# Graph network kernel: fourteen instead of eight pairs of gathered rows before the attention message pass

## The reference, cut to what matters

```
h = x @ W.T                                    # 8 heads of 64
e = leaky_relu(e_src + e_dst) * (1 + et_emb[edge_type]) * edge_weight
e = exp(e - e_max[dst]);  alpha = e / (e_sum[dst] + 1e-10)
msg = h[src] * alpha[:, :, None]
out = zeros.at[dst].add(msg) + x               # then a layer norm
# third layer:
h_self  = x @ W_self.T
h_neigh = mean of x[src] by dst @ W_neigh.T
```

## Time and profile before

| | us |
|---|---|
| median of 3 runs | 1936.45 |
| lowest and highest run | 1935.54, 1938.03 |
| profiled execution, its span | 1934.6 |
| median above the profiled span | 1.85 |
| POOL busy in the whole span | 705.2 |
| POOL gathers for the pass (L693), 176 | 178.6 |
| stage of the attention weights, first POOL gather to last ScalarE copy | 1090.87 to 1134.45 |
| message pass, first ScalarE copy to last matmul | 1135.13 to about 1354.9 |

### The profile page before, as it was taken

The page is one execution under the profiler, slowest core; times in us unless marked ns, Lnnn a source line. Parts: engine busy times, 40 slices in busy tenths (PEclk is TensorE's granted clock), DMA queues, the critical chain, the costliest instruction groups (busy, mean ns, idle before and its releaser), DMA issues. The chain is left out here.

```text
span 1934.6 us, 27686 instructions
## 1 busy us (share of the span) xinstructions
PE 1608.4 (83%) x7565; PEld 981.3 (51%) x7566; DVE 1167.7 (60%) x2310; ACT 471.2 (24%) x884; POOL 705.2 (36%) x605
## 2 busy tenths in 40 slices
PE   6755956776498999998888459998498899999998
PEld 6751633335443555554555435554246545874486
DVE  5779958884365777775467766665774832113222
ACT  4301103432212555554344210000110111001100
POOL 0001877887094776660000347775330010000000
PEclk9997988998698999999899569999799999999999
DMA  0017844005802766682388337776104201430033
GB/s 25 0 47 285 275 136 120 1 1 172 306 27 92 210 197 187 187 169 45 126 317 331 101 100 211 210 209 171 27 1 144 96 1 72 155 122 1 0 136 135
DMA packets 76346, 248.96 MB, mean 129 GB/s; under 512 B 14901, under 2 KB 28582, under 8 KB 68346
## 3 DMA queue, kind: packets, MB, share of 16 engines
q1 hardware_dynamic: 38618, 147.08, 21.1%
q0 software_dynamic: 34592, 96.87, 18.9%
q10 hardware_dynamic: 3072, 4.20, 0.7%
HBM read 215.93 MB, written 32.00 MB: 128 GB/s over the span
## 5 line engine op out<-in xcount | busy, mean ns | idle before, releaser
L664 POOL DMA_INDIRECT tab_slots<-slot_words,slot_address x160 | 238.1, 1488 | 244.5 <-issue 233.3
L693 POOL DMA_INDIRECT e_rows<-tab_h,idx_h x176 | 178.6, 1015 | 293.4 <-POOLq L50 219.8
L1443 PE MATMUL dense_pY<-weights,dense_xT_block 128*128 128x512 f32 x640 | 284.3, 602 | 0.0
L1491 PE MATMUL dense_pY<-parts,dense_number 128*128 128x512 f32 x1000 | 237.7, 399 | 7.1 <-DMA dense_number<-tab_edges_to 7.1
L994 POOL DMA_INDIRECT e_rows<-tab_q,idx_q x192 | 182.0, 948 | 99.4 <-issue 38.9
L1491 PEld LDWEIGHTS dense_pY<-parts,dense_number 128*128 128x128 f32 x1000 | 188.7, 189 | 54.8 <-DMA dense_number<-tab_edges_to 8.6
L787 PE MATMUL e_pS<-e_rows,e_onehot_ring 128*128 128x512 f32 x352 | 194.2, 643 | 22.1 <-DVE e_rows L763 19.2
L1443 PEld LDWEIGHTS dense_pY<-weights,dense_xT_block 128*128 128x128 f32 x640 | 121.9, 194 | 143.1 <-issue 143.1
L1067 PE MATMUL e_pS<-e_rows,e_onehot_f 128*128 128x512 f32 x384 | 181.4, 596 | 0.0
L877 PE MATMUL count_pA<-count_onehot_d,count_onehot_s 128*128 128x512 f16 (+1 forms) x576 | 117.4, 352 | 63.8 <-DVE count_onehot_d L855 60.3
L763 DVE TENSOR_TENSOR e_rows<-e_rows,e_pW 128x1024 f32<-128x1024 f32 x88 | 107.3, 1220 | 69.3 <-DMA e_rows<-tab_h,idx_h 69.0
(11 more groups left out here) (312 smaller groups left out, 2448.4 us busy)
## 6 DMA issues: line engine op xcount, KB each, us to landing
basis_piece<-in_L_gnn_basis_pieces SPq DMA_DIRECT2D x32, 2048.0 KB, 7.9
dense_number<-tab_edges_from SPq DMA_DIRECT2D x20, 1280.0 KB, 5.4
tab_edges_from<-counts_turned SPq DMA_DIRECT2D x10, 1280.0 KB
tab_edges_to<-counts_total SPq DMA_DIRECT2D x10, 640.0 KB
dense_number<-tab_edges_to SPq DMA_DIRECT2D x10, 640.0 KB, 4.6
tab_w<-basis_wout ACTq DMA_DIRECT2D x128, 32.0 KB
weights<-tab_w SPq DMA_DIRECT2D x4, 1024.0 KB, 6.3
weights<-in_L_gnn_W_T SPq DMA_DIRECT2D x3, 1024.0 KB
```

The costliest lines, as they stand in the source:

```text
L664: pool.indirect_dma_start(self.table, bass.IndirectOffsetOnAxis(self.address[:, t:t + 1], 0), self.words[:, t, :], None).then_inc(self.pla ...
L693: pool.indirect_dma_start(self.rows[:, q, s, :], None, self.table, bass.IndirectOffsetOnAxis(self.idx[:, j * 2 + s:j * 2 + s + 1], 0)).the ...
L1443: ins = self.nc.tensor.matmul(self.banks.at(g), self.xt[:, b % 2, c, :], weights[:, c, :], start=c == 0, stop=c == 3)
L1491: ins = self.nc.tensor.matmul(self.banks.at(self.first + b), self.number[:, b % 2, r * NB + k, :], self.parts[r][n][:, k, :], start=k == 0 ...
```

## The change

`RowRing` is given six lent places: halves of W[0], W[1] and W[2], each as large as a ring slot. Pairs 0 to 5 are gathered into these, with semaphores of their own, pairs 6 and 7 into ring slots 6 and 7, and pairs 8 to 13 into ring slots 0 to 5. All 14 pairs (28 indirect DMAs) are issued by POOL within `attention_weights`. The pass's refill begins with pair 14, with the same wait as before. The loads of the third layer's two matrices move from SP's list of `attention_weights` to SP's list of `attention_pass`, where they wait until pairs 0 to 5 are summed; SP waits for them at the end of its list.

```diff
 class RowRing:
-    def __init__(self, nc, ctx, name, table, idx):
+    def __init__(self, nc, ctx, name, table, idx, lent):
...
+        self.got_lent = [sem(f"got_lent{q}") for q in range(len(lent))]
+        self.early = len(lent) + BODYP
+
+    def is_lent(self, i, u):
+        return is_first(i) and u < len(self.lent)
+
+    def rows(self, i, u):
+        return self.lent[u] if self.is_lent(i, u) else self.ring[:, u, :, :]
+
+    def wait_got(self, eng, i, u):
+        if self.is_lent(i, u):
+            eng.wait_ge(self.got_lent[u], 32)
+        else:
+            eng.wait_ge(self.got[u], (i + (0 if u < len(self.lent) else 1)) * 32)

     def gather(self, pool, j):
-        q = j % BODYP
+        i, u = j // BODYP, j % BODYP
         for s in range(2):
-            pool.indirect_dma_start(self.rows[:, q, s, :], None, self.table,
+            pool.indirect_dma_start(self.rows(i, u)[:, s, :], None, self.table,
                                     bass.IndirectOffsetOnAxis(self.idx[:, j * 2 + s:j * 2 + s + 1], 0)
-                                    ).then_inc(self.got[q], 16)
+                                    ).then_inc(self.got_lent[u] if self.is_lent(i, u) else self.got[u], 16)
...
 # attention_pass
         @block.gpsimd
         def _(pool):
-            for j in range(BODYP, PAIRS):
+            for j in range(ring.early, PAIRS):
                 pool.wait_ge(summed, j + 2 - BODYP)
                 ring.gather(pool, j)
+
+        @block.sync
+        def _(sp):
+            sp.wait_ge(summed, len(ring.lent) + 1)
+            for tile, source in fetches:
+                sp.dma_start(tile, source).then_inc(fetched, 16)
+            sp.wait_ge(fetched, 16 * len(fetches))
...
             def multiply(i, u):
-                v.wait_ge(got[u], (i + 1) * 32)
-                r = rows[:, u, :, :].rearrange("p s (h d) -> p s h d", h=H)
+                ring.wait_got(v, i, u)
+                r = rows(i, u).rearrange("p s (h d) -> p s h d", h=H)
...
 # attention_weights
-        @block.sync
-        def _(sp):
-            for tile, source in weights:
-                sp.dma_start(tile, source).then_inc(weights_in, 16)
-            sp.wait_ge(weights_in, 16 * len(weights))
-
         @block.gpsimd
         def _(pool):
-            for j in range(BODYP):
+            for j in range(ring.early):
                 ring.gather(pool, j)
...
 # gnn
-        ring = RowRing(nc, until_dense, "e1", tab["h"], idx["h"])
+        ring = RowRing(nc, until_dense, "e1", tab["h"], idx["h"], [W[n // 2][:, n % 2 * 2:n % 2 * 2 + 2, :] for n in range(6)])
```

More of the change, by code:

```diff
@@ L681, with attention_pass @@
 class RowRing:
-    def __init__(self, nc, ctx, name, table, idx):
-        self.nc, self.table, self.idx = nc, table, idx
+    def __init__(self, nc, ctx, name, table, idx, lent):
+        self.nc, self.table, self.idx, self.lent = nc, table, idx, lent
         sem = stage_semaphores(nc, ctx, name)
-        self.rows = ctx.enter_context(nc.sbuf_tensor(f"{name}_rows", [P, BODYP, 2, D], F32))
+        self.ring = ctx.enter_context(nc.sbuf_tensor(f"{name}_rows", [P, BODYP, 2, D], F32))
         self.got = [sem(f"got{q}") for q in range(BODYP)]
+        self.got_lent = [sem(f"got_lent{q}") for q in range(len(lent))]
[9 more added lines that the diff above has]
+            eng.wait_ge(self.got[u], (i + (0 if u < len(self.lent) else 1)) * 32)
     def gather(self, pool, j):
-        q = j % BODYP
+        i, u = j // BODYP, j % BODYP
         for s in range(2):
-            pool.indirect_dma_start(self.rows[:, q, s, :], None, self.table,
+            pool.indirect_dma_start(self.rows(i, u)[:, s, :], None, self.table,
                                     bass.IndirectOffsetOnAxis(self.idx[:, j * 2 + s:j * 2 + s + 1], 0)
-                                    ).then_inc(self.got[q], 16)
-def attention_pass(nc, name, C, ring, loc, block_turn, block_bank, block_end, acc, weight, side):
+                                    ).then_inc(self.got_lent[u] if self.is_lent(i, u) else self.got[u], 16)
+def attention_pass(nc, name, C, ring, loc, block_turn, block_bank, block_end, acc, weight, side, fetches):
     ns = H + 1
@@ L704, in attention_pass @@
         sem = stage_semaphores(nc, ctx, name)
-        rows, got = ring.rows, ring.got
+        rows = ring.rows
+        fetched = sem("fetched")
         ohr = sb("onehot_ring", [P, 4, 2, P], F32)
@@ L786, in step @@
                     for s in range(2):
-                        nc.tensor.matmul(flat(pS[:, bass.ds(bank[u], 1), :]), ohr[:, u % 4, s, :], rows[:, u, s, :],
+                        nc.tensor.matmul(flat(pS[:, bass.ds(bank[u], 1), :]), ohr[:, u % 4, s, :], rows(i, u)[:, s, :],
                                          start=False, stop=True, skip_group_check=True)
@@ L1907, with attention_weights @@
 L = SLOTS // PAIRS * P
-def attention_weights(nc, name, C, es, ed, factor, loc, block_f, wt, weights, ring):
+def attention_weights(nc, name, C, es, ed, factor, loc, block_f, wt, ring):
     with ExitStack() as ctx:
@@ L1937, in attention_weights @@
         sem = stage_semaphores(nc, ctx, name)
-        weights_in = sem("weights_in")
         s_dve, scored_ready, laid, seq_out, first_out = (
@@ L2280, in gnn @@
             attention_weights(nc, "att", C, es, ed, factor, loc["dst"][:, :], block_of_pair[:, :],
-                              wt, [(W[n][:, :, :], turned_rows(ins, name, 0))
-                                   for n, name in enumerate(("L2_gnn_W_neigh", "L2_gnn_W_self"))], ring)
+                              wt, ring)
         attention_pass(nc, "e1", C, ring, loc["dst"], block_turn, block_bank, block_end, acc, wt,
-                       side)
+                       side, [(W[n][:, :, :], turned_rows(ins, name, 0))
+                              for n, name in enumerate(("L2_gnn_W_neigh", "L2_gnn_W_self"))])
         until_dense.close()
```

## The result

The changed kernel took 1949.51 us (median of 4 runs, 1945.81 to 1956.42) against 1937.24 us of the kernel before (4 runs, 1935.54 to 1939.71): ratio 1.0062 [1.0045, 1.0079], so 0.62% slower. I had forecast 1944.5, in a range to 1948.0. The direction came out as forecast, the median 1.5 us above the range.

A forecast was written before the change was run, and what follows sets the result against it. POOL's gather issue rate, 1.25 us a gather, was taken to bound the pass. A pass starting 10.10 us later, less 2.02 gained, made +8.1 us: 1944.5 us as run median, range 1938.5 to 1948.

The forecast's parts named there:

- The 28 gathers and DVE's hold: Weights stage: DVE's scan and subtraction hold gathers 17 and 18; the 28th gather ends at 1142.17 us.
- The rival in which DVE does not hold them: Weights stage: DVE operations do not lengthen the new gathers; 1937.8 to 1940.2 us, chance 0.13.
- POOL last at the barrier: End of weights stage: POOL's last gather ends 7.72 us behind ScalarE, and PE, DVE and ScalarE wait.
- The price of that barrier: Between weights stage and pass: 3.06 us behind POOL's last gather, lower bound 0.68; pass starts 10.10 us later.
- The gain of 2.0 instead of 15: Pass: twelve fewer gathers free 15.0 us, but the first refill waits for pair 6, 12.98 us later; gain 2.02.
- The loads: Weight loads moved into the pass: land before 1175 us, delay no chain, cost taken as nothing.
- the rival with up to 18 us: Pass: the loads delay the gathers so PE starves early; up to +18 us, 1954.5, chance 0.08.
- DVE's first wait: Pass: DVE first waits for gathered rows near 1197.7 us.
- The cheap barrier: End of weights stage: barrier costs 0.68 us behind POOL too; +5.7 us, 1942.2, chance 0.20.
- gathers that fit in: Weights stage: all 28 gathers fit, or the barrier ignores POOL's queue; 2.0 us faster, 1934.4, chance 0.04.
- the faster side: Pass: deeper stock brings it to PE's pace; 13.5 us faster, 1923, chance 0.03.

The follow-up runs named there:

- The split: Changed kernel, but only 16 gathers in the weights stage and the other 12 at the head of the pass: 1937.84 us, ratio 0.9986.
- second trace of the changed kernel: Changed kernel unaltered, measured again in 12 runs against the kernel before: 1948.13 us, ratio 1.0043.
- 20 gathers: The 16-gather split kernel with ten pairs (20 gathers) issued in the weights stage instead: 1939.22 us, one run.
- POOL's memsets: Kernel before, with 24 chained memsets on POOL behind its 16 gathers in the weights stage: 1945.88 us, one run.
- The run with the ring first: Changed kernel, 28 gathers ahead, but pairs 0 to 7 in the ring, 8 to 13 in lent places; loads behind pair 13, 16 pairs written out: 1949.38 us.
- three versions with new places for the ring: Changed kernel with ring before lent places, 28 gathers ahead (1949.38 us) or 16 (1942.92), or fourteen places used for two rounds (1934.85).
- the longer lists alone: Kernel before, with PE's and DVE's instruction lists of the pass written out for 32 pairs instead of 8: 1943.54 us, ratio 1.0027.

## Why the prediction was right or wrong

**The 28 gathers and DVE's hold: right.** Gathers 17 and 18 were held by the scan and the subtraction. The 17th ended at 1125.88, 0.76 us behind the scan's 1125.12, the 18th at 1128.26, 0.82 behind the subtraction's 1127.44; I had used 0.75 and 0.83. The rival in which DVE does not hold them falls, and with it, for this case, the inference of the Trainium skill (SBUF — State Buffer, "Who interferes with whom").

**POOL last at the barrier, and all the rest waiting: right.** The split takes this away and the whole loss with it.

**The price of that barrier: the step that failed.** The prediction takes 3.06 us for it and keeps 0.68 as the lower bound. It was 4.66 us in the profile of the result, 4.68 in the second trace of the changed kernel, 4.40 with 20 gathers. The 3.06 came from another stage, which POOL leaves last with another indirect DMA (L664, 1.18 us), and was carried over as the same situation. I had named the landing and worked out what it would add, 0.37 us, but put 0.68 us behind it, the price of a barrier that ScalarE leaves last. Behind POOL's memsets with nothing in flight it is 2.22. Landing and that price would have been 1141.22 + 3.7 + 2.22 = 1147.14, 4.97 behind the gather's end, nearer than 3.06. The mechanism was right, the size 1.6 us too small. That alone would not have carried the time out of the range: 1944.5 + 1.6 = 1946.1.

**The gain of 2.0 instead of 15: right in kind, somewhat less in size.** From the start of the pass to the last gather it took 205.31 us instead of 207.02, 1.7 less, and 1.4 less in the second trace. The run with the ring first showed that it is the place that decides: the refill began at 8.3 us instead of 21.2 and paid at pair 22.

**The loads: right.** Landed by 1173.3 against 1175 worked out; alone, they changed the time by 1.0004 [0.999, 1.0018]. The 401 GB/s of that window are nearly twice the 207 of the steady pass, but no chain was waiting then, so the rival with up to 18 us falls.

**DVE's first wait: off, without a price.** 1201.77 instead of 1197.7, with 1.35 us to add for the earlier start and 1.6 to take off for the barrier: the stock lasted some 4 us longer, which no run explains. The steady step was 1.252 us, and PE's pace was not reached: no gather of the 148 came less than 1.24 us behind the one before.

**The rivals that end elsewhere.** The cheap barrier falls to 4.66 us, gathers that fit in to the 7.72 us by which POOL was behind ScalarE, the faster side to the step of 1.25 us.

**The sum and the median.** The forecast was +8.1 us. The stretch gives +9.5 and +10.95 in two executions, 12 runs give 1948.13 - 1939.04 = +9.1, the four runs of the result +12.3. So the forecast was 1 to 2 us short by its barrier term. The rest has two parts. The forecast started from 1936.45, the median of three runs, and the same kernel gave 1937.24 with a fourth and 1939.04 in 35 others; that is scatter of few runs, and without the 2.6 us the twelve runs, at 1948.13, would lie inside the range and not at its end. And the four runs of the result had a median 1.4 us above the twelve, in executions of which no trace exists; twelve runs did not repeat it.

**What stays open.** The first gather of the stretch starts between 1089.5 and 1099.9 us, late in all three versions with new places for the ring (1096.16, 1099.93, 1096.78), which are also three of the four with longer lists. It was late too in the run with 24 memsets (1095.01), but there 3.4 of the 4.1 us had been lost before the stage ahead of the weights stage began. By DVE's first instructions of the two stages, that stage took 143.1, 147.2 and 144.2 us in the three, 138.0 to 141.2 in the kernels with the lists as before, 141.7 with the memsets and 141.8 with the longer lists alone. As that last trace is of an execution that shows none of its version's loss, it doesn't clear the longer lists; they, the places and the loads behind a later pair stay as rivals. In the three the basis loads of that stage took 8.2 to 8.6 us to land (median), with the longer lists alone 8.0, and 7.7 to 7.9 in the kernel before, the changed one and the split, whose first gathers came at 1089.5 to 1091.9. I can't tell cause from company. Nor can I say where the written-out lists lose their 0.27%.

## What to carry to other kernels

A prefetch ahead of a barrier is free only while its queue is not the last one there. POOL had 11.65 us in hand and was given 12 gathers of at least 1.25 us, two of them held much longer, so it came 7.7 us late, and a barrier behind gathers in flight cost 4.66 us instead of 0.66. The same gathers issued at the head of the next stage cost nothing that could be measured. And before more places are lent, ask into which place the first refill goes: places used once at the front push the refill back by as many pairs as they hold, and gave 1.7 of 15 us; the same places used for two rounds gave 9.6 us in the stretch, of which 3.8 reached the time of the kernel.

## What the runs showed of the hardware that was not expected

- A barrier has a price by who comes last and with what: 0.66 us behind ScalarE's copies, 2.22 behind POOL's memsets, 4.40 to 4.68 behind POOL's indirect gathers. It reaches back, too: with POOL's last gather over 2.30 us before ScalarE was through, the barrier still cost 2.10 instead of 0.66.
- The last pairs land more slowly. Near the end of the pass DVE's multiplies start 2.7 to 3.6 us apart, always waiting for rows, while POOL issues a pair every 2.5 us:

```profile
1342.98 1.22 DVE L785 TENSOR_TENSOR e_rows<-e_rows,e_pW 128x1024 f32<-128x1024 f32 x1 [1.83 <-DMA e_rows<-tab_h,idx_h]
1346.57 1.22 DVE L785 TENSOR_TENSOR e_rows<-e_rows,e_pW 128x1024 f32<-128x1024 f32 x1 [2.03 <-DMA e_rows<-tab_h,idx_h]
1349.91 1.22 DVE L785 TENSOR_TENSOR e_rows<-e_rows,e_pW 128x1024 f32<-128x1024 f32 x1 [1.79 <-DMA e_rows<-tab_h,idx_h]
```

  The DMA engines move 160 GB/s from 1339 to 1351, with a share of 0.87, instead of 207 with 0.73. In the kernel before the same begins some 10 us earlier, about as far ahead of its last gather (166 GB/s from 1326 to 1346), so it goes with the last ten or so gathers and not with the change. Why isn't shown; that these hold much of the padding (the 20000 edges would fill 78.1 of the 88 pairs) was not tested. So the 9.1 us behind the last gather are more than a landing and a multiply: from its start to the last multiply 8.52 us in the changed kernel, 9.08 in the one before.
